# Causal attention cores: several heads' narrow score tiles in one bank, and value products in two visits a group

## The chip, the cores and the metric

The kernel runs on one core of a Trainium2 chip. Its time is the device time of one execution in microseconds; the profile is one execution taken by the hardware profiler. Of the core's engines, TensorE (PE) multiplies, VectorE (DVE), ScalarE (ACT) and GpSimd (POOL) do the element-wise work, and SyncE (SP) and ACT issue transfers. Matrix products land in eight banks of PSUM, each 512 fp32 columns wide. The engines run their own instruction streams in order and meet at semaphores.

## The reference

One decoder layer on x of 4 batches, 512 rows, 512 columns: causal self-attention (16 heads of 32), cross-attention to a context (32 heads of 16), then a second causal self-attention with rotary positions (16 heads of 32), then a gated mixture of experts. The change touches the cores of the two causal attentions:

```python
scores = jnp.einsum('bqhd,bkhd->bhqk', q, k)
scores = jnp.where(causal_mask[None, None], scores, NEG)
attn = jax.nn.softmax(scores, axis=-1)
out = jnp.einsum('bhqk,bkhd->bqhd', attn, v).reshape(b, s, HIDDEN)
return out @ w_out
```

## The kernel before

Phases follow one another: for each attention a projection phase and a core phase, then the experts. `core_phase` is built three times, as "first" and "rotary" (both causal) and as "cross". A causal core goes through 16 groups: four batches of four groups, a group being four heads of one batch. Each group has 16 steps; step i stands for key block m = i // 4 (128 keys) and head j = i % 4 of the group.

In each step PE first makes a tile of plain scores for a later group (`scores`, L1158), 26 steps ahead, into one of three banks (0, 1, 2). DVE takes that tile's row maxima with the mask added (`tile_max`, L1385), and only then is the bank free again: a tile of scores waits for the maximum of the tile three before it. When a group's 16 maxima are there, POOL splits them into two parts (`split_max`, L1584 and L1586), PE turns them at step 8 of the group before (`max_transpose`, L1172), ACT copies them out (L1311) and sends them with a transfer (`send_max`, L1093) into rows of the group's stack of queries. These rows subtract the maximum inside the product of the transposed scores, so step 0 of the group waits for the transfer.

Then the step makes its tile of transposed scores (`scoresT`, L1192): 128 keys by the queries from block m on, so 512, 384, 256 or 128 columns for m = 0, 1, 2, 3. A second product of 128 columns (L1195, the identity times a triangle of large negative numbers) adds the mask to the diagonal block. ACT takes the exponential out of the bank (L1339). These tiles share three banks (3, 4, 7) in turn with the turned maxima and with the output projection; `share_banks` replays the order and notes, for each use, the semaphore by which the bank's last user has left it.

The value products (`values`, L1233) take four heads side by side in four strips of 32 columns of the array, with fp32 operands; so do the products with a column of ones (L1201) that give the softmax's sums: one for query block 0 from the exponentials themselves (`sums_of_first`), one for blocks 1 to 3 (`sums`) from a total that POOL adds up (`add_keys`, L1566). I call a stretch in which PE leaves the wide products for such narrow strips a visit. A group's value products of blocks 0, 1, 2, 3 stand at its steps 9 and 13 and at steps 1 and 5 of the next group, the sums of block 0 behind the first of them and the other sums at step 4 of the next group: five visits. DVE turns the sums at step 5 (`flip_sums`, L1400), inverts them and turns them back at step 6 (L1407, L1410), and scales the values at step 7 (`scale`, L1420), between tile maxima. The next group's value product of block 0 waits for this scaling.

From its second batch on, a core also projects a finished batch in thirds of four products (`project`, L1250), in the second and third group of a batch: for tile m at steps 6, 7, 10 (m even) or 12, 14, 15 (m odd). I call these six groups of a core projecting groups and the other ten plain groups.

SP loads the stacks three groups ahead. A load waits until all transposed scores of the group that had the slot are done.

Of the kernel before, what the change touches and what calls it, by code (L numbers as in the profile page):

```python
# [24 lines left out]
P = 128  # L25
B, S, D = 4, 512, 512
# [888 lines left out]
def core_phase(nc, s, c, psum, a):  # L915
# [11 lines left out]
    with ctx:  # L927
# [56 lines left out]
        VALUES_LAG, SUMS_STEP = 7 if cross else 9, 4  # L984
# [18 lines left out]
        def values_behind(g, step):  # L1003

            n, beat = divmod(g * N16 + step - VALUES_LAG, HEADS_AT_ONCE)
            return divmod(n, TT) if beat == 0 and 0 <= n < GROUPS * TT else None
# [20 lines left out]
        def share_banks():  # L1027
# [14 lines left out]
            for g in range(GROUPS):  # L1042
                for step in range(N16):
                    n = g * N16 + step
                    whole(("score", n), "exp_done", n + 1)
# [12 lines left out]
        with nc.Fori(0, B // BODY) as loop:  # L1058
            rows = lambda m, bi: m[bass.ds((loop * BODY + bi) * S, S), :].rearrange("(t p) d -> p t d", p=P)
            with nc.Block() as block:  # L1060
# [86 lines left out]
                def _(pe):  # L1147
# [28 lines left out]
                    def scoresT(g, i):  # L1176

                        m, j = divmod(i, HEADS_AT_ONCE)
                        n, slot = g * N16 + i, g % STACK_SLOTS
                        at, r = j // HALVES, j % HALVES * HALF_ROWS  # L1180
                        bank, q0 = psum[bank_at["score", n]], start_k(m)
                        if i == 0:
# [95 lines left out]
                    for g in range(GROUPS):  # L1278
                        for step in range(N16):
# [6 lines left out]
                            if values_behind(g, step):  # L1286
                                g_v, m_v = values_behind(g, step)
                                values(g_v, m_v)
                                if causal and g_v == GROUPS - 1:
                                    sums_at_end(m_v)  # L1290
                                elif causal and m_v == 0:
                                    sums_of_first(g)
                            if causal and g and step == SUMS_STEP:
                                sums(g - 1)
                            if projected_at(g, step):
                                project(*projected_at(g, step))
                    for step in range(VALUES_LAG):
                        if values_behind(GROUPS, step):
                            g_v, m_v = values_behind(GROUPS, step)
# [6 lines left out]
                def _(act):  # L1306
# [18 lines left out]
                    for g in range(GROUPS):  # L1325
                        for step in range(N16):
                            n = g * N16 + step
                            q0 = start_k(step // HEADS_AT_ONCE)
                            act.wait_ge(s.scoresT_ready, n + 1)
# [1163 lines left out]
```

## Time and profile before

| what | us |
|---|---|
| median of 3 runs (lowest, highest) | 2136.97 (2126.91, 2140.46) |
| the profiled execution | 2134.5 |
| its span | 2132.7 |
| PE busy, share of the span | 1982.2, 93% |
| DVE busy | 1356.2, 64% |
| ACT busy | 1046.5, 49% |
| POOL busy | 706.1, 33% |

The two causal cores lie at about 176 to 432 us and 1184 to 1440 us. A matmul's busy time in the trace overlaps with its neighbours' (its end is modelled), so costs on PE are read from one start to the next. A row of the timeline may merge several records; x8 on a value product is four heads with two records each. A bracket such as [0.37 <-DVE ...] is time in which the engine sat idle before the row, and what ended it.

### The profile page before, as it was taken

The numbers are of one execution on the slowest core, as the hardware profiler recorded it, in microseconds if no ns is written. First come the engines' busy times: TensorE is split into PE (matmuls) and PEld (weight loads), VectorE is DVE, ScalarE is ACT, GpSimd is POOL, SyncE is SP. The second block draws the span as 40 slices with busy tenths as digits, with TensorE's granted clock in tenths as the row PEclk, the third lists the DMA queues.
The fourth block names the chain that finished last, engine by engine and source line by source line (L and its number), as shares of the span: only waits on it lengthen the run. The fifth ranks groups of instructions, "written<-read, shape, count | busy, mean of one in ns | idle before, by whom it ended". The sixth has DMA issues, their size and how long they took to land. (4 is left out here: it accounts for less than half of the span.)

```text
span 2132.7 us, 32709 instructions
## 1 busy us (share of the span) xinstructions
PE 1982.2 (93%) x10991; PEld 1385.6 (65%) x10991; DVE 1356.2 (64%) x2805; ACT 1046.5 (49%) x1890; POOL 706.1 (33%) x610
## 2 busy tenths in 40 slices
PE   7998999968789999998899899998999999999998
PEld 6875666656533334343777566666787888787876
DVE  6455666557689897976778566645331325577775
ACT  3424554445368676865443455534322221476775
POOL 0003655436512332323466465531000000143433
PEclk9998999989889999999999799998999999999999
DMA  5637676247665545443474867626120206434342
GB/s 202 223 141 183 149 170 153 91 163 268 233 180 119 141 113 140 119 104 95 188 242 181 203 153 164 149 81 245 45 99 1 79 25 254 171 67 76 64 77 37
DMA packets 151994, 297.75 MB, mean 140 GB/s; under 512 B 24722, under 2 KB 43284, under 8 KB 150740
## 3 DMA queue, kind: packets, MB, share of 16 engines
q1 hardware_dynamic: 114052, 242.29, 38.1%
q10 hardware_dynamic: 29040, 34.74, 6.0%
q0 software_dynamic: 8736, 18.62, 4.8%
q8 instruction: 89, 1.46, 0.3%
q14 instruction: 77, 0.63, 0.1%
HBM read 181.55 MB, written 102.50 MB: 133 GB/s over the span
## 5 line engine op out<-in xcount | busy, mean ns | idle before, releaser
L1339 ACT ACTIVATE cross_c_prob<-bank 128x512 f32<-128x512 f32 x512 | 271.1, 599 | 116.7 <-PE bank L1192 115.4
L1389 DVE TENSOR_REDUCE row_max<-bank 128x2 f32<-128x1024 f32 x248 | 290.6, 1211 | 27.6 <-PE bank L1158 26.6
L1859 PE MATMUL bank<-moe_hT,moe_w 128*128 128x512 f32 x1056 | 250.1, 393 | 7.7 <-DVE moe_w L2148 7.7
L1192 PE MATMUL bank<-stack 56*128 56x512 f32 (+4 forms) x768 | 232.9, 428 | 7.0 <-ACT cross_c_prob L1339 3.1
L1859 PEld LDWEIGHTS bank<-moe_hT,moe_w 128*128 128x128 f32 x1056 | 199.1, 189 | 50.1 <-issue 8.1
L1158 PE MATMUL bank<-stack 48*128 48x512 f32 (+4 forms) x720 | 190.7, 443 | 25.6 <-PEq L71 13.7
L1192 PEld LDWEIGHTS bank<-stack 56*128 56x128 f32 (+1 forms) x768 | 118.5, 193 | 136.4 <-ACT cross_c_prob L1339 69.6
L1339 ACT ACTIVATE first_c_prob<-bank 128x512 f32<-128x512 f32 (+3 forms) x256 | 106.1, 436 | 120.1 <-PE bank L1195 117.1
L1339 ACT ACTIVATE rotary_c_prob<-bank 128x512 f32<-128x512 f32 (+3 forms) x256 | 105.6, 436 | 117.8 <-PE bank L1195 115.2
L1385 DVE CUSTOM_DVE_ANT_0 first_c_masked<-bank,later 128x128 f32<-128x128 f32 (+3 forms) x240 | 108.8, 485 | 77.8 <-PE bank L1158 77.1
L1158 PEld LDWEIGHTS bank<-stack 48*128 48x128 f32 (+1 forms) x720 | 93.3, 196 | 98.4 <-DVE row_max L1389 45.1
L1385 DVE CUSTOM_DVE_ANT_0 rotary_c_masked<-bank,later 128x128 f32<-128x128 f32 (+3 forms) x240 | 108.5, 485 | 70.3 <-PE bank L1158 69.6
L2273 DVE TENSOR_TENSOR moe_prod<-moe_prod,bank 128x512 f32<-128x512 f32 x44 | 30.2, 687 | 179.2 <-PE bank L1859 179.2
L1233 PE MATMUL bank<-cross_c_prob,cross_c_v 128*32 128x512 f32 x1024 | 138.1, 612 | 0.6 <-DVE cross_c_flipped L1400 0.6
L1870 PE MATMUL bank<-moe_w,moe_inner 128*128 128x512 f32 x528 | 128.8, 393 | 0.0
L1797 POOL TENSOR_TENSOR moe_res<-moe_res,moe_x_tile 128x512 f32<-128x512 f32 x16 | 21.8, 1362 | 312.7 <-DMA moe_x_tile<-x 312.7
L1195 PE MATMUL bank<-earlier_r,ident_r 128*128 128x128 f32 x512 | 123.5, 242 | 0.0
L1817 POOL DMA_INDIRECT out_x<-moe_res,moe_token x39 | 61.8, 1585 | 173.1 <-ACT moe_res L2068 171.2
L1870 PEld LDWEIGHTS bank<-moe_w,moe_inner 128*128 128x128 f32 x528 | 98.7, 188 | 21.0
L2038 ACT ACTIVATE moe_prod<-bank 128x512 f32<-128x512 f32 x44 | 26.3, 598 | 172.6 <-PE bank L1859 172.6
L1969 PE MATMUL bank<-moe_down_w_e,moe_innerT 128*128 (+1 forms) x234 | 107.2, 593 | 1.5 <-issue 1.5
L1195 PEld LDWEIGHTS bank<-earlier_r,ident_r 128*128 128x128 f32 x512 | 101.6, 198 | 6.4
(402 smaller groups left out, 4482.6 us busy)
## 6 DMA issues: line engine op xcount, KB each, us to landing
qk_parts<-first_p_parts SPq DMA_DIRECT2D x32, 512.0 KB, 2.6
stack<-qk_parts SPq DMA_DIRECT2D x64, 256.0 KB, 6.4
qk_parts<-cross_p_parts SPq DMA_DIRECT2D x32, 512.0 KB, 2.6
stack<-qk_parts SPq DMA_DIRECT2D x256, 64.0 KB, 2.6
qk_parts<-rotary_p_parts SPq DMA_DIRECT2D x32, 512.0 KB, 2.7
moe_gate_up_e<-in_experts_gate_up SPq DMA_DIRECT2D x8, 1408.0 KB, 9.1
moe_raw<-in_shared_packed SPq DMA_DIRECT2D x11, 768.0 KB, 8.5
stack<-qk_parts SPq DMA_DIRECT2D x16, 512.0 KB, 5.3
```

What stands on the lines that cost most here:

```text
L1158: last = nc.tensor.matmul(bank[:, 0 : width_q(m)], q_stack[slot][r : r + PRODUCT_ROWS, at, m * P : (m + 1) * P], k_stack[slot][r : r + PRO ...
L1192: last = nc.tensor.matmul(bank[:, 0 : S - q0], k_stack[slot][r : r + ALL_ROWS, at, m * P : (m + 1) * P], q_stack[slot][r : r + ALL_ROWS, a ...
L1195: last = nc.tensor.matmul(bank[:, 0:P], c.ident_r[:], c.earlier_r[:], start=False, stop=True)
L1233: last = nc.tensor.matmul(psum[bank_o][32 * j : 32 * j + 32, q0:S], val, probability(g, m, j), start=m == 0, stop=m == TT - 1)
L1339: nc.scalar.activation(probability(g, step // HEADS_AT_ONCE, step % HEADS_AT_ONCE), psum[bank_at["score", n]][:, 0 : S - q0], ACT.Exp).the ...
L1385: nc.vector.tensor_tensor_reduce(out=masked[:, n % 2, 0 : width_q(m)], in0=bank[:, 0 : width_q(m)], in1=c.later[:, S - width_q(m) : S], sc ...
L1389: nc.vector.tensor_reduce(row_max[:, g % 2, m, j - 1 : j + 1], c.banks[:, first : first + WIDE, :], AX_X, ALU.max).then_inc(s.max_done, 1)
L1817: pool.indirect_dma_start(a.out, bass.IndirectOffsetOnAxis(ap=token[:, t : t + 1], axis=0), y[:, t % 2, :], None, bounds_check=B * S - 1, ...
L1859: last = nc.tensor.matmul(psum[bank][:], weights(pa, f, k), hT[p % 2][:, pb, k, :], start=m == 0, stop=m == len(steps) - 1)
L1870: last = nc.tensor.matmul(psum[SD[t]][:], inner[:, n % 2, pa, t * P : (t + 1) * P], w_d(pb, f), start=f == 0 and m == 0, stop=f == KF - 1 ...
L1969: last = nc.tensor.matmul(psum[6 + t % 2][:], innerT[0:kn, t % 2, n, :], rhs, start=n == 0, stop=n == len(FE_K) - 1)
L2273: nc.vector.tensor_tensor(prod[:], prod[:], psum[SU][:], ALU.mult).then_inc(s.s_inner, 1)
```

## The change

Tiles of transposed scores of key block 2 (256 columns) are made for two heads in one bank, those of block 3 (128 columns) for four heads in one bank. The bank gets one mask product for all its heads, of 256 or 512 columns (the triangle read again for each head), and one exponential of 512 columns. So steps 8, 10 and 12 lead, and steps 9, 11, 13, 14 and 15 make no transposed scores. The value products of blocks 0 and 1, with the sums of block 0, stand at step 13; those of blocks 2 and 3, with the other sums behind them, at step 4 of the next group. The cross-attention's order is as before.

```diff
+        PACKED = {2: 2, 3: 4} if causal else {}
+        heads_in = lambda step: PACKED.get(step // HEADS_AT_ONCE, 1)
+        leads = lambda step: step % heads_in(step) == 0
-        VALUES_LAG, SUMS_STEP = 7 if cross else 9, 4
+        VALUES_LAG = 7
+        VALUES_AT = {13: (0, (0, 1)), 4: (1, (2, 3))}
...
+            if causal:
+                back, tiles = VALUES_AT.get(step, (0, ()))
+                return [(g - back, m) for m in tiles if g >= back]
...
-                    whole(("score", n), "exp_done", n + 1)
+                    if leads(step):
+                        whole(("score", n), "exp_done", n + heads_in(step))
...
-                        last = nc.tensor.matmul(bank[:, 0 : S - q0], k_stack[slot][r : r + ALL_ROWS, at, m * P : (m + 1) * P],
-                                                q_stack[slot][r : r + ALL_ROWS, at, q0:S], start=True, stop=not causal)
+                        for h in range(heads):
+                            at, r = (j0 + h) // HALVES, (j0 + h) % HALVES * HALF_ROWS
+                            last = nc.tensor.matmul(tiles[:, h], k_stack[slot][r : r + ALL_ROWS, at, m * P : (m + 1) * P],
+                                                    q_stack[slot][r : r + ALL_ROWS, at, q0:S], start=h == 0, stop=not causal)
                         if causal:
-                            last = nc.tensor.matmul(bank[:, 0:P], c.ident_r[:], c.earlier_r[:], start=False, stop=True)
-                        last.then_inc(s.scoresT_ready, 1)
+                            last = nc.tensor.matmul(tiles[:, :, 0:P], c.ident_r[:], c.earlier_r[:].unsqueeze(1).to_broadcast([P, heads, P]), start=False, stop=True)
+                        last.then_inc(s.scoresT_ready, heads)
...
-                            if values_behind(g, step):
-                                g_v, m_v = values_behind(g, step)
+                            for g_v, m_v in values_behind(g, step):
                                 values(g_v, m_v)
                                 if causal and g_v == GROUPS - 1:
                                     sums_at_end(m_v)
-                                elif causal and m_v == 0:
-                                    sums_of_first(g)
-                            if causal and g and step == SUMS_STEP:
-                                sums(g - 1)
+                                elif causal and m_v == 1:
+                                    sums_of_first(g_v)
+                                elif causal and m_v == TT - 1:
+                                    sums(g_v)
...
+                            if causal and leads(step):
+                                nc.scalar.activation(prob_of[m][:, j : j + heads], psum[bank_at["score", n]][:, 0 : heads * (S - q0)].rearrange("p (h n) -> p h n", h=heads),
+                                                     ACT.Exp).then_inc(s.exp_done, heads)
```

PE before, from step 12's transposed scores to step 15 of a plain group (L1158 plain scores of the later group, L1192 transposed scores, L1195 mask, L1233 values of block 1):

```order
L1192 MATMUL bank<-first_q_stack,first_k_stack 128x128
L1195 MATMUL bank<-earlier_r,ident_r 128x128
L1158 MATMUL bank<-stack 128x256
L1192 MATMUL bank<-first_q_stack,first_k_stack 128x128
L1195 MATMUL bank<-earlier_r,ident_r 128x128
L1233 MATMUL bank<-first_c_prob,first_c_v 32x384 x4
L1158 MATMUL bank<-stack 128x384
L1192 MATMUL bank<-first_q_stack,first_k_stack 128x128
L1195 MATMUL bank<-earlier_r,ident_r 128x128
L1158 MATMUL bank<-stack 128x384
L1192 MATMUL bank<-first_q_stack,first_k_stack 128x128
L1195 MATMUL bank<-earlier_r,ident_r 128x128
```

PE with the change, from step 11 to step 0 of the next group (the same products are now L1166, L1204, L1207, L1245, and the sums L1213):

```order
L1166 MATMUL bank<-stack 128x256 x2
L1204 MATMUL bank<-first_q_stack,first_k_stack 128x128 x4
L1207 MATMUL bank<-earlier_r,ident_r 128x512
L1166 MATMUL bank<-stack 128x256
L1245 MATMUL bank<-first_c_prob,first_c_v 32x512 x4
L1245 MATMUL bank<-first_c_prob,first_c_v 32x384 x4
L1213 MATMUL bank<-first_c_prob,ones 32x128 x4
L1166 MATMUL bank<-stack 128x384 x3
```

The four masks of block 3 have become one, the four tiles stand together at step 12, and the values of block 0 have moved from step 9 to stand right ahead of those of block 1. Behind them three tiles of plain scores follow one another with nothing between.

PE before, steps 4 and 5 of a group (L1201 the sums, L1233 the values of block 3 of the group before; those of block 2 stood at step 1):

```order
L1158 MATMUL bank<-stack 128x512
L1192 MATMUL bank<-stack 128x384
L1195 MATMUL bank<-earlier_r,ident_r 128x128
L1201 MATMUL bank<-first_c_total,ones 32x384 x4
L1158 MATMUL bank<-stack 128x512
L1192 MATMUL bank<-stack 128x384
L1195 MATMUL bank<-earlier_r,ident_r 128x128
L1233 MATMUL bank<-first_c_prob,first_c_v 32x128 x4
```

PE with the change, steps 4 and 5:

```order
L1166 MATMUL bank<-stack 128x512
L1204 MATMUL bank<-first_q_stack,first_k_stack 128x384
L1207 MATMUL bank<-earlier_r,ident_r 128x128
L1245 MATMUL bank<-first_c_prob,first_c_v 32x256 x4
L1245 MATMUL bank<-first_c_prob,first_c_v 32x128 x4
L1213 MATMUL bank<-first_c_total,ones 32x384 x4
L1166 MATMUL bank<-stack 128x512
```

Three visits have become one at step 4: blocks 2 and 3 and the sums behind each other. The turn of the sums on DVE still follows at step 5, now behind the values of block 3 too.

## Rows read from the trace of the kernel before

**Rows 1.** the page, part 4: the chain of work that ended last, by engine.

```profile
PE 40%; DMA 1%; DVE 1%; issue 1%; POOL 1%; ACT 1%; SPq 0%; DVEq 0%; ACTq 0%; POOLq 0%
```

**Rows 2.** stretches from one turn of the maxima to the next: us, busy us of each engine.

```profile
core 0: us, PE busy (x) PEld busy (x) DVE busy (x) ACT busy (x) POOL busy (x), PEclk, DMA share, GB/s
354.51:367.17 12.66, 12.18 (x102) 8.22 (x101) 9.16 (x37) 7.40 (x19) 8.79 (x6) 1.00 0.96 213
367.17:381.45 14.28, 13.91 (x111) 9.72 (x110) 10.41 (x41) 7.75 (x19) 9.31 (x7) 1.00 0.40 90
381.45:399.04 17.59, 17.39 (x124) 12.45 (x124) 10.38 (x34) 7.84 (x18) 8.69 (x7) 1.00 0.46 148
```

**Rows 3.** PE in order of time, early plain group: start us, us, line, tiles, shape.

```profile
355.78 1.07 PE L1233 MATMUL bank<-first_c_prob,first_c_v 128*32 128x512 f32 x8 [0.37 <-DVE first_c_attn L1420]
356.63 0.43 PE L1201 MATMUL bank<-first_c_prob,ones 128*32 128x128 f32 x8
356.99 0.39 PE L1158 MATMUL bank<-stack 96*128 96x256 f32 x1
...
357.75 0.33 PE L1158 MATMUL bank<-stack 96*128 96x256 f32 x1
357.92 0.22 PE L1192 MATMUL bank<-first_q_stack,first_k_stack 104*128 104x128 f32 x1
357.98 0.28 PE L1195 MATMUL bank<-earlier_r,ident_r 128*128 128x128 f32 x1
358.09 0.33 PE L1158 MATMUL bank<-stack 96*128 96x256 f32 x1
...
358.33 0.27 PE L1195 MATMUL bank<-earlier_r,ident_r 128*128 128x128 f32 x1
358.53 0.85 PE L1233 MATMUL bank<-first_c_prob,first_c_v 128*32 128x384 f32 x8
359.31 0.45 PE L1158 MATMUL bank<-stack 96*128 96x384 f32 x1
359.59 0.23 PE L1192 MATMUL bank<-first_q_stack,first_k_stack 104*128 104x128 f32 x1
```

**Rows 4.** instruction groups by shape: weight loads of transposed scores; values of block 0.

```profile
L1192 PEld LDWEIGHTS bank<-stack 104*128 104x128 f32 x256 | 52.2, 204 | 5.5 <-DMA stack<-first_c_max_rows 2.0 <-DMA stack<-rotary_c_max_rows 1.4
...
L1233 PE MATMUL bank<-first_c_prob,first_c_v 128*32 128x512 f32 x128 | 18.8, 659 | 3.1 <-DVE first_c_attn L1420 2.6 <-ACT first_c_prob L1339 0.5
```

**Rows 5.** DVE in order of time, same group, from the turn of the sums.

```profile
352.34 0.72 DVE L1400 STREAM_TRANSPOSE first_c_flipped<-bank 128x512 f32<-128x512 f32 x1 [0.29 <-PE bank L1201]
...
353.60 0.29 DVE L1385 CUSTOM_DVE_ANT_0 first_c_masked<-bank,later 128x128 f32<-128x128 f32 x1
...
354.73 0.25 DVE L1385 CUSTOM_DVE_ANT_0 first_c_masked<-bank,later 128x128 f32<-128x128 f32 x1
...
354.94 0.69 DVE L1420 TENSOR_TENSOR first_c_attn<-bank,first_c_flipped 128x512 f32<-128x512 f32 x1
355.55 0.28 DVE L1385 CUSTOM_DVE_ANT_0 first_c_masked<-bank,later 128x128 f32<-128x128 f32 x1
...
357.42 0.42 DVE L1385 CUSTOM_DVE_ANT_0 first_c_masked<-bank,later 128x256 f32<-128x256 f32 x1 [1.37 <-PE bank L1158]
```

**Rows 6.** all engines in order of time: maxima split, then turned.

```profile
353.99 0.22 POOL L1586 TENSOR_TENSOR first_c_max_parts<-row_max,first_c_max_parts 128x16 fp32r<-128x16 f32 x1
...
354.51 0.60 PE L1172 MATMUL bank<-ident,first_c_max_parts 128*8 128x128 f32 x4
```

**Rows 7.** all engines in order of time: maxima sent, and who waited.

```profile
355.76 0.73 ACTq L1093 DMA_DIRECT2D stack<-first_c_max_rows  x1
...
360.67 0.19 PEld L1192 LDWEIGHTS bank<-stack 104*128 104x128 f32 x1 [0.37 <-DMA stack<-first_c_max_rows]
```

**Rows 8.** the same two operations one batch earlier.

```profile
292.31 0.71 ACTq L1093 DMA_DIRECT2D stack<-first_c_max_rows  x1
...
298.32 0.19 PEld L1192 LDWEIGHTS bank<-stack 104*128 104x128 f32 x1 [1.47 <-DMA stack<-first_c_max_rows]
```

More of the change, by code:

```diff
@@ L1003, in values_behind @@
         def values_behind(g, step):
+            if causal:
+                back, tiles = VALUES_AT.get(step, (0, ()))
+                return [(g - back, m) for m in tiles if g >= back]
             n, beat = divmod(g * N16 + step - VALUES_LAG, HEADS_AT_ONCE)
-            return divmod(n, TT) if beat == 0 and 0 <= n < GROUPS * TT else None
+            return [divmod(n, TT)] if beat == 0 and 0 <= n < GROUPS * TT else []
         def probability(g, m, j):
@@ L1176, in scoresT @@
                     def scoresT(g, i):
-                        m, j = divmod(i, HEADS_AT_ONCE)
-                        n, slot = g * N16 + i, g % STACK_SLOTS
-                        at, r = j // HALVES, j % HALVES * HALF_ROWS
+                        if not leads(i):
+                            return
+                        m, j0 = divmod(i, HEADS_AT_ONCE)
+                        n, slot, heads = g * N16 + i, g % STACK_SLOTS, heads_in(i)
                         bank, q0 = psum[bank_at["score", n]], start_k(m)
+                        tiles = bank[:, 0 : heads * (S - q0)].rearrange("p (h n) -> p h n", h=heads)
                         if i == 0:
@@ L1297, in _ @@
                     for step in range(VALUES_LAG):
-                        if values_behind(GROUPS, step):
-                            g_v, m_v = values_behind(GROUPS, step)
+                        for g_v, m_v in values_behind(GROUPS, step):
                             if causal:
@@ L1327, in _ @@
                             n = g * N16 + step
-                            q0 = start_k(step // HEADS_AT_ONCE)
-                            act.wait_ge(s.scoresT_ready, n + 1)
+                            m, j = divmod(step, HEADS_AT_ONCE)
+                            q0, heads = start_k(m), heads_in(step)
+                            if leads(step):
+                                act.wait_ge(s.scoresT_ready, n + heads)
                             if cross and n >= PROB_SLOTS:
@@ L1338, in _ @@
                                     act.wait_ge(s.sums_done, 2 * g - 1)
-                            nc.scalar.activation(probability(g, step // HEADS_AT_ONCE, step % HEADS_AT_ONCE), psum[bank_at["score", n]][:, 0 : S - q0],
-                                                 ACT.Exp).then_inc(s.exp_done, 1)
+                            if causal and leads(step):
+                                nc.scalar.activation(prob_of[m][:, j : j + heads], psum[bank_at["score", n]][:, 0 : heads * (S - q0)].rearrange("p (h n) -> p h n", h=heads),
+                                                     ACT.Exp).then_inc(s.exp_done, heads)
+                            if cross:
+                                nc.scalar.activation(probability(g, m, j), psum[bank_at["score", n]][:, 0:S], ACT.Exp).then_inc(s.exp_done, 1)
                             if step == MAX_STEP and g + 1 < GROUPS:
```

## The prediction

> **What bounds the kernel.** I read the chain of waits first: PE holds 40% of the span and no other engine or transfer over 1% (the rest is issue and small shares) [rows 1]. Next the stretches between two turns of the maxima in the first core's last batch: in a plain stretch of 12.66 us PE is busy 12.18, DVE 9.16; with output projection in it, 14.28 and 17.59 us, PE busy 13.91 and 17.39 [rows 2]. The reader is to see that PE sets the pace of a causal core, that DVE is at 72% of a plain stretch and at 59% of the longest, and that the clock is granted in full there. So time taken off PE counts, unless another engine is then late. Where that can be is read from the timelines of PE and DVE.
>
> **Mask products.** The kernel drops from 16 to 11 a group: four masks of 256-column tiles become two of 256 columns, four masks of 128-column tiles become one of 512. The columns streamed are the same, 16 x 128. So the gain is only what a narrow product costs beyond its columns. From mask to mask neighbours: plain scores of 256 columns, transposed scores of 128 and mask of 128 take 358.09 - 357.75 = 0.34 us for 512 columns [rows 3]; a value product of 512 columns in fp32 takes 0.85 us at four passes, so 512 columns are 0.21 us. That leaves 0.13 us for three products; weight loads with only 128 columns to hide behind show, one narrow product costing 0.11 us instead of 0.06. I price a mask at 0.11 us, 256 columns at 0.12 and 512 at 0.23. Then 8 x 0.11 - 2 x 0.12 - 0.23 = 0.41 us a group less. Bounds: 0 (only columns cost) and 0.55 (five products at 0.11). The four narrow score tiles in a row stay at 0.11 each, as now. I take 0.41, the price of the nearest rows.
>
> The Trainium skill, "TensorE: Matmul & The Clock Gate", section "Back-to-back issue gap", speaks against this term: its isolated gap is N/2.4 + 2.5 ns, by which eight masks of 128 columns and their three successors differ by some 12 ns a group. By that estimate the term would be 0; the 0.34 us of the row speaks against it.
>
> **Visits.** Five a group become two. Leaving one costs: values of 384 columns last 359.31 - 358.53 = 0.78 us to the next product, of which 0.64 is streaming (0.75 of 0.85), so 0.14; where sums follow values nothing is added (356.63 - 355.78 = 0.85). The 128-column sums show the same: 356.99 - 356.63 = 0.36, of which 0.21 is streaming. The first wide product after it is also late, 359.59 - 359.31 = 0.28 us for 384 columns against 0.22 that the 0.17 of 256 columns plus 0.05 would give. Entering costs 358.53 - 358.33 = 0.20 behind a mask worth 0.11 [rows 3]. Together 0.14 + 0.06 + 0.08 = 0.28 us a visit, 0.84 a group. Bounds 0.14 and 0.35 a visit.
>
> **The wait for the scaled values.** Values of block 0 waited 0.37 us for DVE's scaling [rows 3], 2.6 us in total in the first core [rows 4], which is seven times, so in plain groups. At step 13 the scaling is some 4 us old. This wait goes: 0.37 a plain group.
>
> **What comes late instead.** The visit at step 9 was also DVE's time to catch up. After the turn of the sums at 352.34 DVE works without a pause: maximum 0 at 353.60, maximum 1 at 354.73, the scaling at 354.94 to 355.55, then maxima 2 and 3 at 0.21 us each, done by 355.97; then it waits 1.37 us for PE, which is in the visit [rows 5]. With the change PE has no visit from step 5 to step 12. Each tile of scores waits for the maximum three before. The turn of the maxima cannot come earlier than the split of the last ones allows (POOL ends at 354.21, PE turned at 354.51 [rows 6]), so say 354.3. Then 0.36 for the turn and 0.11 for tile 3: tile 4 could start at 354.77, but maximum 1 is done at 354.94, and semaphore and weight load add some 0.15: 355.10, a wait of 0.33. Tile 4, two transposed tiles and a mask take 0.48: tile 5 at 355.58, maximum 2 is done at 355.76, so 355.91, 0.33 more. Tile 6 waits another 0.09. With 0.2 at the turn itself and 0.1 where tile 11 follows the three tiles in a row of steps 14, 15 and 0, that is 1.05 us in a plain group. Bounds: 0.4 (latency of a semaphore nothing) and 1.6 (every wait twice its latency). In projecting groups thirds of 0.9 us stand between these steps and cover them; I leave 0.1 us, for a bank that the projection holds.
>
> **The maxima's transfer.** It is issued 1.25 us behind the turn, 355.76 against 354.51, and in this group it released PE 4.9 us later, after a wait of 0.37 us [rows 6, 7]; in the batch before it took 6.0 us and PE waited 1.47 [rows 8]. In both causal cores weight loads of transposed scores waited 2.0 and 1.4 us on it [rows 4], so in most groups it had landed by the time PE came. PE came at 360.30 in rows 7 if it had not waited: 4.54 us behind the issue. With the change: 5.79 us from turn to step 0, less 0.37, 0.28 and 0.41, plus 0.75 of the new waits behind the turn: 5.48, or 4.23 behind the issue, 0.3 us less room. The groups that wait now lose 0.3 each, in all 2 us; the others nothing, or up to 0.3 if they land just in time. The stack loads that share the DMA engines can start earlier, since the last transposed scores now end at step 12, and so be out of the way earlier; I count nothing for that.
>
> The Trainium skill, "DMA: Bandwidth & Descriptors", section "Anatomy of one DMA", gives 2.0 us and bytes at 436 GB/s, an estimate of 2.2 us for these 64 KB; by it no group would wait. The 4.9 and 6.0 us of the trace disagree.
>
> **Other engines at no cost.** ACT's exponentials of block 2 and 3 become three of 512 columns instead of eight narrow ones; ACT is busy 7.40 of 12.66 us [rows 2] and loses work. The first exponential of block 2 is longer by 0.2 us ahead of the copy of the maxima, and ends before the turned maxima are there. The POOL totals end some 1 us before step 4's sums; the visit's values stand ahead of them. If that cover were gone, a late total would cost PE its lateness, once a group.
>
> **Sum.** Plain group: 0.41 + 0.84 + 0.37 - 1.05 = 0.57 us. Projecting group: 0.41 + 0.84 - 0.1 = 1.15. A core has ten and six: 5.7 + 6.9 = 12.6 us, two cores 25, less 2 for the transfer: 23 us. The profiled execution took 2134.5 us, so 2111.5; it lies 2.5 below the median of the three runs, inside their spread. I forecast **2111 us**, 1.2% less. About 1% (21 us, so 2116) is what a measurement of this kernel can tell from no change.
>
> **Rivals.**
> - Full gain: the waits on maxima do not come, because DVE's order leaves PE just behind it. For: DVE has 28% to spare on average. Against: the pauseless stretch of rows 5. Gain 2 x (10 x 1.62 + 6 x 1.25) - 2 = 45 us: 2089. Chance 0.12.
> - DVE eats the plain groups: waits of 1.6 us leave nothing of 1.62 there, and only projecting groups gain, 2 x 6.9 = 14 us, less the 2: 2122. For: three banks only, and each late release also uncovers a weight load. Chance 0.18.
> - The merged masks do nothing, as the columns are the same. Then 32 x 0.41 = 13 us less gain: 2124. For: equal columns, and a triangle read four times with a stride of zero, which no row shows. Against: the 0.34 us. Chance 0.14.
> - Slower: the maxima's transfer becomes the bound. Its place is step 0, and from 4.23 us behind the issue on each us is PE's. If the earlier stack loads now fall on it in every plain group and it takes the 6.0 us of rows 8, 20 groups wait 1.8 us, 36 us against the 25 gained: 2146. Turning point: 5.5 us. At 7 us it would be 20 x 2.8 - 25 = 31 slower, 2166. Against: only three or so groups a core wait now, and loads start earlier. Chance 0.08.
> - Forecast: 0.48.
>
> **Chances and range.** Faster by over 1% (below 2116): 0.41 of the forecast, the full gain 0.12, 0.03 of the masks' case: 0.56. Slower by over 1%: 0.04. The rest, 0.40, is within. The range runs from near the full gain to short of the slower case, 2092 to 2131: it leaves out most of the slower case, part of the full gain, and the worst of DVE's bound.
>
> **What would show it.** In the profile after: 352 mask products, their mean below 0.3 us; two runs of L1245 a group, the second with sums at its end; no wait of PE on the scaled values; waits of L1166's weight loads on row maxima longer in total than before, at steps 8 to 12 of plain groups; plain stretches near 12.0 us and stretches with projection 1 to 1.4 us shorter. I would be wrong if PE's idle time at step 0 grows by a us, or if plain stretches stay at 12.6.

## The result, and the profile after

| | median of the runs, us | lowest, highest |
|---|---|---|
| before | 2138.72 (4 runs) | 2126.91, 2142.66 |
| the change | 2106.87 (4 runs) | 2101.05, 2111.76 |

The ratio is 0.9859, 95% interval 0.9812 to 0.9906: 30 us faster by the ratio. The same kernel was measured once more, with six runs, beside three of the experiments.

> The change itself once more, on the same chip as the three runs beside it. Ratio to before 0.983 to 0.989. If the length of its waits for the maxima's transfer is a matter of one execution, the records show another sum than the 10 us of the first profile.

It took 2109.24 us, ratio 0.9882 (0.9857 to 0.9907). Its record shows 6.2 us of PE waiting for the maxima's transfer in the causal cores, where the first one shows 10.2 (below): the sum of these waits differs by 4 us between two executions of one kernel, so a single record of another kernel says little by it. The profiled execution that is shown in the following is the slowest of the first four, 2111.76 us with a span of 2110.0.

The page's line of the engines (busy us, share, instructions), and of its part 4 the chain of work that ended last:

```profile
PE 1963.1 (93%) x10831; PEld 1381.2 (65%) x10831; DVE 1353.1 (64%) x2805; ACT 1022.5 (48%) x1730; POOL 706.1 (33%) x610
PE 40%; DMA 2%; issue 1%; DVE 1%; POOL 1%; ACT 1%; SPq 0%; DVEq 0%; ACTq 0%; POOLq 0%
```

PE is busy 19.1 us less than before (1982.2, with 160 products more), and the span is 22.7 us shorter. It still holds 40% of the chain, and DMA has 2% where it had 1 [rows 1].

Stretches from one turn of the maxima to the next, in the first core, in a view restricted to PE: the stretch, its length, PE's busy us (and instructions), granted clock, DMA engines' share, GB/s. First the kernel before, in stretches without a wait for the maxima's transfer: a plain one, the one into the first projecting group, and the two projecting ones.

```profile
230.57:242.87 12.30, 11.93 (x102) 1.00 0.86 194
242.87:256.97 14.10, 13.73 (x110) 1.00 0.87 204
320.44:338.37 17.93, 17.73 (x127) 1.00 0.49 117
338.37:354.51 16.14, 15.94 (x118) 1.00 0.53 134
```

The same four kinds with the change, and behind them the plain stretch that ends a batch, at 347.52 us:

```profile
233.18:244.91 11.73, 11.53 (x98) 1.00 0.75 171
244.91:258.32 13.41, 13.21 (x105) 1.00 0.89 193
316.16:332.68 16.52, 16.45 (x121) 1.00 0.49 121
332.68:347.52 14.84, 14.77 (x113) 1.00 0.56 146
347.52:362.18 14.66, 13.19 (x98) 0.88 1.08 219
```

The first four are 12.30, 14.10, 17.93 and 16.14 us before and 11.73, 13.41, 16.52 and 14.84 after: 0.57, 0.69, 1.41 and 1.30 less, 3.97 in a batch of four groups. The fifth is 14.66 long, its clock is granted at 0.88, and it was 12.66 before [rows 2]: two us worse. Each of the four kinds gets shorter where there is no wait for the transfer; some of the stretches that have one get longer.

PE in that last plain group, from the turn of the maxima to the next group's first transposed scores (x2 and x4 are tiles that the view has merged):

```profile
347.52 0.60 PE L1180 MATMUL bank<-ident,first_c_max_parts 128*8 128x128 f32 x4
347.88 0.77 PE L1166 MATMUL bank<-stack 96*128 96x128 f32 x2
348.49 0.40 PE L1204 MATMUL bank<-first_q_stack,first_k_stack 104*128 104x256 f32 x2
348.72 0.28 PE L1207 MATMUL bank<-earlier_r,ident_r 128*128 128x256 f32 x1
349.10 0.59 PE L1166 MATMUL bank<-stack 96*128 96x256 f32 x2
349.54 0.56 PE L1204 MATMUL bank<-first_q_stack,first_k_stack 104*128 104x128 f32 x4
349.93 0.45 PE L1207 MATMUL bank<-earlier_r,ident_r 128*128 128x512 f32 x1
350.21 0.28 PE L1166 MATMUL bank<-stack 96*128 96x256 f32 x1
350.42 1.71 PE L1245 MATMUL bank<-first_c_prob,first_c_v 128*32 128x512 f32 x16
351.95 0.40 PE L1213 MATMUL bank<-first_c_prob,ones 128*32 128x128 f32 x8
352.28 0.79 PE L1166 MATMUL bank<-stack 96*128 96x384 f32 x3
354.37 0.50 PE L1204 MATMUL bank<-stack 104*128 104x512 f32 x1 [1.30 <-DMA stack<-first_c_max_rows]
```

DVE at the same time: maximum 1, the scaling, maximum 2:

```profile
347.94 0.25 DVE L1400 CUSTOM_DVE_ANT_0 first_c_masked<-bank,later 128x128 f32<-128x128 f32 x1
...
348.15 0.69 DVE L1435 TENSOR_TENSOR first_c_attn<-bank,first_c_flipped 128x512 f32<-128x512 f32 x1
348.76 0.28 DVE L1400 CUSTOM_DVE_ANT_0 first_c_masked<-bank,later 128x128 f32<-128x128 f32 x1
...
348.96 0.08 DVE L1400 DVE_READ_ACCUMULATOR2_ANT row_max<- 128x1 f32 x1
```

The merged row at 347.88 holds tiles 3 and 4 of plain scores, and the next row begins at 348.49: 0.61 us for two narrow tiles priced at 0.11 each. Tile 4 waited for maximum 1, done when the scaling starts at 348.15. Tile 5 follows the mask of 348.72 and was due 0.12 later, at 348.84; it stands at 349.10, behind maximum 2, whose last row starts at 348.96. Tiles 5 and 6 then take 0.44 to the next row instead of 0.24, as tile 6 waits for maximum 3. These are the three waits of the forecast's list: 0.39, 0.26 and 0.20 us by the distances of starts, against 0.33, 0.33 and 0.09. At 352.28 three tiles of 384 columns run on, and PE then stands idle 1.30 us for the transfer.

The groups by shape (count | busy us, mean ns | idle us ahead): the value products of block 0, which waited for DVE 2.6 us [rows 4] and do so no more, and the masks:

```profile
L1245 PE MATMUL bank<-first_c_prob,first_c_v 128*32 128x512 f32 x128 | 17.9, 633 | 0.1
...
L1207 PE MATMUL bank<-earlier_r,ident_r 128*128 128x128 f32 x256 | 60.3, 235 | 0.0
L1207 PE MATMUL bank<-earlier_r,ident_r 128*128 128x256 f32 x64 | 18.8, 294 | 0.0
L1207 PE MATMUL bank<-earlier_r,ident_r 128*128 128x512 f32 x32 | 14.9, 465 | 0.0
```

The masks are 352, with a mean of (60.3 + 18.8 + 14.9) / 352 = 0.27 us, where 512 had one of 0.24. PE's waits for the maxima's transfer over the whole execution: us in total, times, longest.

```profile
PE bank L1204 <- DMA stack<-first_c_max_rows: 5.5, 3, 3.2
PE bank L1204 <- DMA stack<-rotary_c_max_rows: 4.7, 3, 1.9
PE bank L1204 <- DMA stack<-cross_c_max_rows: 1.3, 3, 0.8
```

That is 10.2 us in six waits of the causal cores; before, the same two lines had 1.2 and 0.6 us, in one wait each. Four of the six stand at the ends of the second and third batch of each core (0.96, 1.30, 1.88 and 1.37 us, 5.5 together). The other two, 3.20 and 1.47 us, stand at the second group of each core, where there was none before. The longer one:

```profile
195.47 0.65 PE L1204 MATMUL bank<-stack 104*128 104x512 f32 x1 [3.20 <-DMA stack<-first_c_max_rows]
```

The stretch of turns around it takes 18.52 us where it took 13.40, which is the largest single loss in this record; in the second record of the change it takes 14.40, without such a wait.

### The profile page after: what moved, and what is told of

Read it like the earlier page. It is cut to its first block and busy times, and to the rows that moved or that the text cites. A ratio compares the mean times of both kernels' runs of the same rounds, so it can differ in the third digit from the quotient of the medians.

```text
span 2110.0 us, 32325 instructions
## 1 busy us (share of the span) xinstructions
PE 1963.1 (93%) x10831; PEld 1381.2 (65%) x10831; DVE 1353.1 (64%) x2805; ACT 1022.5 (48%) x1730; POOL 706.1 (33%) x610
## 5 line engine op out<-in xcount | busy, mean ns | idle before, releaser
L1204 PE MATMUL bank<-stack 56*128 56x512 f32 (+4 forms) x768 | 224.0, 433 | 15.0 <-DMA stack<-first_c_max_rows 5.5
L1166 PE MATMUL bank<-stack 48*128 48x512 f32 (+4 forms) x720 | 184.7, 442 | 26.9 <-PEq L71 13.5
L1204 PEld LDWEIGHTS bank<-stack 56*128 56x128 f32 (+1 forms) x768 | 114.3, 195 | 143.7 <-ACT cross_c_prob L1355 69.1
L1352 ACT ACTIVATE rotary_c_prob<-bank 128x512 f32<-128x512 f32 (+1 forms) x176 | 94.1, 559 | 122.4 <-PE bank L1207 122.1
L1352 ACT ACTIVATE first_c_prob<-bank 128x512 f32<-128x512 f32 (+1 forms) x176 | 94.0, 558 | 120.9 <-PE bank L1207 118.2
L1166 PEld LDWEIGHTS bank<-stack 48*128 48x128 f32 (+1 forms) x720 | 92.7, 197 | 90.9 <-DVE row_max L1404 46.1
L1245 PE MATMUL bank<-cross_c_prob,cross_c_v 128*32 128x512 f32 x1024 | 137.2, 608 | 0.6 <-DVE cross_c_flipped L1415 0.6
L1207 PE MATMUL bank<-earlier_r,ident_r 128*128 128x128 f32 (+2 forms) x352 | 94.0, 267 | 0.0
L2328 DVE SCALAR_TENSOR_TENSOR moe_chunks<-moe_gate_up_e,moe_w_ln,moe_chunks 128x704 fp32r<-128x704 f32 x78 | 74.0, 951 | 27.0 <-ACT moe_chunks L2098 26.7
```

Source lines behind the costliest of these rows:

```text
L1166: last = nc.tensor.matmul(bank[:, 0 : width_q(m)], q_stack[slot][r : r + PRODUCT_ROWS, at, m * P : (m + 1) * P], k_stack[slot][r : r + PRO ...
L1204: last = nc.tensor.matmul(tiles[:, h], k_stack[slot][r : r + ALL_ROWS, at, m * P : (m + 1) * P], q_stack[slot][r : r + ALL_ROWS, at, q0:S] ...
L1207: last = nc.tensor.matmul(tiles[:, :, 0:P], c.ident_r[:], c.earlier_r[:].unsqueeze(1).to_broadcast([P, heads, P]), start=False, stop=True)
L1245: last = nc.tensor.matmul(psum[bank_o][32 * j : 32 * j + 32, q0:S], val, probability(g, m, j), start=m == 0, stop=m == TT - 1)
L1352: nc.scalar.activation(prob_of[m][:, j : j + heads], psum[bank_at["score", n]][:, 0 : heads * (S - q0)].rearrange("p (h n) -> p h n", h=he ...
```

## Experiments

Ratios are to the kernel before, with 95% intervals. The stretches named are those of the four kinds above, in that order, without a wait for the transfer.

**Only the packing.**

```diff
-        VALUES_LAG = 7
-        VALUES_AT = {13: (0, (0, 1)), 4: (1, (2, 3))}
+        VALUES_LAG, SUMS_STEP = 7 if cross else 9, 4
...
-            if causal:
-                back, tiles = VALUES_AT.get(step, (0, ()))
-                return [(g - back, m) for m in tiles if g >= back]
```

> Shared banks, merged masks and exponentials as in the change, but the value products and sums at their old steps (five visits a group). If a narrow mask product costs more than its columns, as the forecast priced it (0.41 us a group), this is 13 us faster than before, 2125 against 2138, ratio 0.994, and PE's waits on row maxima stay near those of before, since the visit at step 9 still covers DVE. If only columns cost, it is within 3 us of before, ratio 0.999 to 1.001.

Measured: 2114.78 us, 0.992 (0.9888 to 0.9951), 17 us faster; weight loads of plain scores waited 51.3 us on row maxima, near the 47.8 of before. A plain and a projecting stretch of it, and its value products of block 0:

```profile
230.81:243.11 12.30, 11.77 (x98) 1.00 0.77 176
316.62:333.63 17.01, 17.01 (x121) 1.00 0.52 127
```

```profile
L1242 PE MATMUL bank<-first_c_prob,first_c_v 128*32 128x512 f32 x128 | 17.9, 631 | 5.0 <-DVE first_c_attn L1432 4.5 <-ACT first_c_prob L1349 0.5
```

A plain stretch gains nothing: PE arrives at step 9 earlier, and the wait for the scaled values grows from 2.6 to 4.5 us. The gain is in the projecting stretches, 17.93 to 17.01. PE's waits there for the copies of finished output tiles, 1.4 us a core in six waits before, are gone from its list, 0.23 us a projecting group. By that the 0.21 us which merged masks save in a plain group (the run with one mask product a head, below) go into the wait for the scaled values, which grew by 1.9 us over the ten plain groups of a core.

**Only the two visits.**

```diff
-        PACKED = {2: 2, 3: 4} if causal else {}
+        PACKED = {}
```

> Two visits a group as in the change, but every head's transposed tile in its own bank with its own mask and exponential. If the forecast's price of a visit (0.28 us) and of the waits that take their place holds, this is 12 to 18 us faster than before, ratio 0.992 to 0.994. If the visits' gain is wholly eaten by waits on row maxima and on the maxima's transfer, it is within 4 us of before.

Measured: 2123.4 us, 0.9958 (0.9938 to 0.9978), 9 us faster (5 to 13 by the interval): less than the 12 to 18 expected and more than the rival's 4, with an interval that only touches the first and just misses the second. Its plain and projecting stretches:

```profile
228.47:240.55 12.08, 11.79 (x101) 1.00 0.88 197
317.21:334.61 17.40, 17.18 (x126) 1.00 0.51 121
```

Plain 12.08, projecting 17.40. The four kinds together: packing alone gives 1.93 us a batch, visits alone 1.49 (12.08, 13.63, 17.40 and 15.87), both together 3.97. In a plain stretch neither does much alone, 0 and 0.22, and both give 0.57: each alone leaves PE at a wait that both together don't have. With the packing alone it is the scaled values. With the visits alone PE's list has 4.0 us in 15 waits for row maxima of the causal cores, which neither before nor the change has, and still the 2.8 us for copies of output tiles. That these waits are the whole of the difference was read from the lists and not tested.

**One mask product a head.**

```diff
-                            last = nc.tensor.matmul(tiles[:, :, 0:P], c.ident_r[:], c.earlier_r[:].unsqueeze(1).to_broadcast([P, heads, P]), start=False, stop=True)
+                            for h in range(heads):
+                                last = nc.tensor.matmul(tiles[:, h, 0:P], c.ident_r[:], c.earlier_r[:], start=False, stop=h == heads - 1)
```

> The change with shared banks and merged exponentials, but the mask product made for each head by itself (128 columns each, 16 a group instead of 11). If the narrow products' overhead is what the packing brings on PE, this loses 13 us against the change: 2120, ratio to before 0.992. If the columns alone cost, or if what packing brings is fewer waits on banks and on ACT, it stays at 2107, ratio 0.986.

Measured: 2115.8 us, 0.9907 (0.9878 to 0.9936). Stretches 11.94, 13.67, 16.87 and 15.21: 0.21, 0.26, 0.35 and 0.37 longer than the change's, 0.30 on average. So five mask products cost 0.30 us at equal columns, 0.06 each, and 0.07 each in the projecting stretches, where PE is hardly interrupted. By the stretches that is some 9 us in 32 groups, where 13 were expected. The time agrees, 9 us over the first median of the change and 7 over the second, but the intervals overlap; the stretches decide.

**One more visit.**

```diff
-        VALUES_AT = {13: (0, (0, 1)), 4: (1, (2, 3))}
+        VALUES_AT = {13: (0, (0,)), 14: (0, (1,)), 4: (1, (2, 3))}
```

> The change with the value products of block 1 (and the sums behind them) one step later than those of block 0, so that one tile of plain scores stands between: three visits a group instead of two, everything else as it was. By the forecast's price a stretch without a transfer wait gets 0.28 us longer, 9 us in all: ratio to before 0.991. If only the drain of 0.14 us counts, because the product behind a visit is late for its weights anyway, it is 0.14 a stretch, 4 us, 0.989.

Measured (four runs): 2110.23 us, 0.9891 (0.9844 to 0.9939), too near to the change for the time to tell. The stretches tell: 16.82 and 15.14 in projecting groups, 0.30 more each; 11.82 and 13.52 in the others, 0.10 more each. The additional visit costs 0.30 us in the projecting stretches and 0.1 in the others. That it costs less there because the next tiles wait for maxima anyway is an explanation and not shown.

**Small stack loads.**

```diff
         n = next(sent)
+        if t.causal and g >= STACK_SLOTS:
+            last, src = first + 1, src[0:1]
```

> The change, with each load of a causal stack from the fifth group on shrunk to its first row (the later groups so compute on the first groups' stacks; the output is not the reference's). If the maxima's transfer is late because the stack loads share the DMA engines with it, PE's waits on it (10 us in the two cores' records) vanish, with the slow clock behind them: 8 to 14 us faster than the change, ratio to before 0.980 or so. If the transfer's own latency is the bound, the waits stay and the time is that of the change, 0.986.

Measured: 2099.75 us, 0.9844 (0.9813 to 0.9875), 7 us less than the change's first median and 3 by the ratios, 9 and 8 against the second, with the intervals overlapping. That is the lower end of the expected 8 to 14 us or short of it, and its interval leaves out the 0.980. The waits did vanish: in its record PE waits for no transfer of the causal cores, neither at the ends of batches nor at their start, and the plain stretch that ends a batch has the length of any other:

```profile
343.26:354.96 11.70, 11.52 (x97) 1.00 0.29 77
```

11.70 instead of 14.66 us, and the DMA engines' share at 0.29 instead of 1.08. The transfer's own latency leaves PE no wait; with the full loads beside it there is one.

**The scaling three steps later.**

```diff
-        FLIP_STEP, NORM_STEP, BACK_STEP = (4, 6, 8) if cross else (5, 6, 7)
+        FLIP_STEP, NORM_STEP, BACK_STEP = (4, 6, 8) if cross else (5, 6, 10)
```

> The change with DVE's scaling of the values at step 10 instead of 7, so that maxima 2 and 3 of a group no longer stand behind it. If PE's waits for those maxima are what the change gave back in plain groups (0.46 us at tiles 5 and 6), a plain stretch without a transfer wait goes from 11.7 to 11.3 us and 20 groups give 6 to 9 us, unless PE then stands at the maxima's transfer: ratio to before 0.982. If those waits are hidden by something else, no change against the run beside it.

Measured: 2111.35 us, 0.9888 (0.9861 to 0.9916), the same as the change beside it (0.9882). Its plain stretches without and with a wait for the transfer:

```profile
231.25:242.59 11.34, 11.24 (x98) 1.00 0.77 163
346.02:362.08 16.06, 14.19 (x98) 0.79 1.07 209
```

The waits for maxima 2 and 3 are gone where they were expected (11.34 against 11.73), and the end of a batch takes it back: 16.06 against 14.66, at a granted clock of 0.79, with waits for the transfer of 9.1 us in the causal cores. The stretches gain as expected. The expected 0.982 lies outside the interval; the record shows the gain going into the transfer.

**Earlier turn of the maxima.**

```diff
-        MAX_STEP = 9 if cross else 8
+        MAX_STEP = 9 if cross else 6
...
-out=x1, lead=10, **layer)
+out=x1, lead=12, **layer)
```

> The change with the plain scores two steps further ahead (28 instead of 26) and the turn of the maxima at step 6 instead of 8, so that their transfer is issued some 0.9 us of PE work earlier. If the room between the transfer's issue and step 0 is short by what the records show (10 us of waits, and the slow clock behind the longest), the waits drop to a third and this is 6 to 10 us faster than the change: ratio 0.981. If the transfer is late for a reason that moves with it, or if PE now waits for the split of the maxima instead, nothing or a loss of a few us.

Measured: 2102.61 us, 0.9862 (0.9839 to 0.9885); waits for the transfer 5.2 us instead of the 6.2 of the change beside it, which is no drop to a third and within what two executions differ by. It is 7 us below the change beside it only by medians, and the two intervals overlap. PE's waits for POOL's split, one in each core, grew from 4.7 us to 6.7, as the rival said.

**Both.** 

> Scaling at step 10 and the earlier turn together. If both theories hold and the two do not share one wait, their gains add: 12 to 18 us faster than the change, ratio 0.978. If the earlier turn alone mattered, as the run with it alone.

Measured: 2102.46 us, 0.9858 (0.9834 to 0.9882). The gains do not add: its waits for the transfer are 8.2 us, more than the 6.2 of the change beside it, and those for POOL's split 6.1. That PE with its shorter stretches comes to the transfer earlier is the likely reason; the expected 0.978 is outside the interval.

**Stores behind the loads.** Where the change's waits at the ends of batches come from is in SP's own rows. SPq is SP's queue; L1119 is the store of a projected tile, L213 a stack's loads (five a stack; the first of one stack is shown and the first of the next), ACTq's L1101 the maxima's transfer; the last row is the weight load of PE that it released:

```profile
335.94 6.58 SPq L1119 DMA_DIRECT2D x<-first_c_out_t  x2
342.56 0.59 SPq L213 DMA_DIRECT2D first_q_stack<-qk_parts  x1
...
348.87 0.73 ACTq L1101 DMA_DIRECT2D stack<-first_c_max_rows  x1
...
350.41 0.59 SPq L213 DMA_DIRECT2D first_q_stack<-qk_parts  x1
...
354.37 0.19 PEld L1204 LDWEIGHTS bank<-stack 104*128 104x128 f32 x1 [1.61 <-DMA stack<-first_c_max_rows]
```

The same time by stretches of PE, columns as above:

```profile
340.00:343.00 3.00, 3.00 (x17) 1.00 0.00 0
346.00:355.00 9.00, 7.53 (x60) 1.00 1.09 240
357.00:359.00 2.00, 2.00 (x20) 0.50 1.06 208
```

SP's row of two stores lasts from 335.94 to 342.52: the second one waits for a tile whose last third is projected at step 15 of the batch's third group, and the next stack's loads are issued behind it, at 342.56. From 340 to 343 the DMA engines move no byte. From 346 to 355 they are full (share 1.09), with the loads of the stack after it issued 7.9 us later, at 350.41. The maxima's transfer, issued at 348.87 between the two, releases PE 5.5 us later. Behind the wait PE gets half its clock for 357 to 359, the level of 1.2 GHz.

Before, the loads of the same two stacks were issued so:

```profile
349.30 0.59 SPq L213 DMA_DIRECT2D first_q_stack<-qk_parts  x1
...
360.36 0.59 SPq L213 DMA_DIRECT2D first_q_stack<-qk_parts  x1
```

The first came 5.2 us ahead of the turn at 354.51, with the change 5.0: behind the store it gains nothing from slots that are free at step 12. The second came 4.6 us behind the transfer's issue, and with the change comes 1.5 behind it. The transfer itself hardly changed: at the four batch ends of the two cores it released PE 4.9 to 6.0 us behind its issue before, 5.4 on average, and 5.2 to 6.1 with the change, 5.6 on average. What shrank is PE's way: the weight load of step 0 would have come 4.54 us behind the issue before, and comes 3.89 behind it with the change, at each of the four places.

```diff
                             next_stack(sp, g + 3)
+                        if causal and g > G and OUT_AT[3][-1][0] >= (g - 1) % G >= OUT_AT[1][-1][0]:
+                            store(sp, ((g - 1) // G - 1) * TT + [m for m in range(TT) if OUT_AT[m][-1][0] == (g - 1) % G][-1])
...
-                        for m in early:
+                        for m in early[:-1] if causal else early:
```

> The change with SP's second store of each projecting group (which waits for the output of step 10 or 15) put behind the next stack's loads instead of ahead of them. In the change's record SP waits in that store from 336 to 342.5 us, no byte moves from 340 to 343, and then two stacks' loads fall on the maxima's transfer. If that is what makes the transfer late at the end of a batch, the stretches of 14.7 us there go to 12 to 13, four or so in the two cores: 5 to 9 us faster than the change, ratio 0.983. If the loads merely take their 1.5 MB a group wherever they start, nothing.

Measured: 2094.55 us, 0.9831 (0.9797 to 0.9864), the ratio that was expected: 12 and 15 us below the change's two medians, 6 and 11 by the ratios, with intervals that overlap. SP's and ACT's rows at the same place:

```profile
328.90 0.59 SPq L213 DMA_DIRECT2D first_q_stack<-qk_parts  x1
...
334.75 0.34 SPq L1119 DMA_DIRECT2D x<-first_c_out_t  x1
...
341.45 0.73 ACTq L1101 DMA_DIRECT2D stack<-first_c_max_rows  x1
...
342.98 0.59 SPq L213 DMA_DIRECT2D first_q_stack<-qk_parts  x1
```

A stack's loads now start 11.2 us ahead of the turn of the maxima (328.90 against 340.10; 5.0 in the change), ahead of the store of 334.75, and 14.1 us before those of the next stack. At the issue of the maxima's transfer, 341.45, the DMA engines have little else to do (share 0.07 from 341.4 to 343.0, where it is over 1 at this place in the change), and the stretch at the end of the batch is an ordinary one, 11.76 us instead of 14.66:

```profile
340.10:351.86 11.76, 11.57 (x98) 1.00 0.76 174
```

The other three batch ends are the same, 11.75 to 11.77 us, where the change has 12.75 to 16.58 in its first record and 12.87 to 14.45 in its second. PE waits at none of them. The move doesn't touch the wait at the second group of a core; in this record it is 1.7 us in the second core and nothing in the first.

**All three.** 

> Scaling at step 10, plain scores two further ahead with the turn at step 6, and the stores behind the loads. If the transfer is the bound once PE has been relieved, this adds the gains the two former runs could not show: ratio 0.979 to 0.982, 2090 to 2095. If the loads' bytes are the bound in any order, it stays at 2102, ratio 0.986.

Measured: 2089.76 us, 0.9803 (0.9768 to 0.9837): 42 us under the kernel before by the ratio, as expected. Its ratio is below both intervals of the change (0.9812, 0.9857 at their lower ends), though its own interval still overlaps the first a little. This is the fastest by its median of the versions that compute everything; the run with the stores alone is within its interval. A projecting and a plain stretch:

```profile
321.35:337.50 16.15, 16.15 (x121) 1.00 0.69 167
337.50:348.54 11.04, 11.04 (x97) 1.00 0.69 149
```

Only the plain one can be held against those above: with the turn at step 6 a stretch holds other thirds of the projection.

**Both moves with small loads.** 

> Scaling at step 10 and the earlier turn, with the causal stack loads from the fifth group on shrunk to their first row (the output is not the reference's). If the loads are the only thing that stands against those two moves, PE never waits for the transfer and the plain stretches are all 11.0 to 11.3 us: ratio 0.975 to 0.979, 8 us or more below the run with both moves. If PE is then held by something else, it is no better than the change with small loads, 0.984.

Measured: 2091.55 us, 0.981 (0.9777 to 0.9843), short of the 0.979, and 11 us below the run with both moves, as expected. Its plain stretches are 11.03 us as expected, but it has no more to gain in the steady part than the kernel with all three; one wait of 4.6 us for POOL's split in each core's first groups is what it still has.

## Why the prediction was right

The forecast was 2111 us and 1.2% less; measured were 2107 and 1.4%. Its range held the time. The terms for PE's own work are borne out in kind, but the nearness of the sum is partly luck: more was gained in the projecting groups than forecast and more lost at the transfer.

- **Mask products**, 0.41 us a group: measured 0.30 (0.21 in plain, up to 0.37 in projecting ones). Right that columns are not all; but the merged mask of block 3 takes 0.28 us to the next start (349.93 to 350.21) where I had 0.23, half of what is missing. The rival by which merged masks do nothing is refuted. The Trainium skill's isolated gap ("TensorE: Matmul & The Clock Gate", section "Back-to-back issue gap") makes this term an estimate of next to nothing; the trace does not agree, with its 0.30. The same section says that the isolated gap counts too little for narrow products in a stream, and gives 81 ns at 128 columns and 131 ns at 512 there, which the forecast left out. By these, with 256 columns between the two, the term is an estimate of 0.26 to 0.36 us. The 0.30 agrees with that difference, though not with the two figures: the rows have 0.11 us [rows 3] and 0.28.
- **Visits**, 0.28 us each: an additional one costs 0.30. The trace agrees with the term's unit. Three fewer did not give 0.84 everywhere: from packing alone to the full change a projecting stretch gains 0.49 and 0.30 us, where the forecast's terms give 0.74. What stands in the rest was not found.
- **The wait for the scaled values**, 0.37: gone. That packing alone makes it longer was not foreseen.
- **The waits on maxima**, 1.05: at tiles 4, 5 and 6 the changed kernel shows them in the places given, 0.85 us for the three where I had 0.75, and putting the scaling later took 0.39 back in a plain stretch. Wrong was one sign named for it: weight loads' waits on row maxima would grow in total, I said. In the causal cores they fell, from 21.2 + 13.3 + 13.3 = 47.8 us to 11.5 + 8.2 + 7.1 = 26.8. Where a wait ends is the better sign than a sum.
- **A term that was missing**: with eleven tiles of scores a group in place of sixteen, PE hardly waits for a copy of a projected tile to free a bank: 2.8 us in both cores before, 0.4 now. Packing alone gives a projecting stretch 0.92 and 1.00 us, of which masks are 0.35 and 0.37 and the bank's waits 0.23; 0.34 and 0.40 are left unexplained. The projecting stretches so gained 1.41 and 1.30 where I had 1.15, the stretch between the two kinds 0.69. A batch came to 3.97 us against 3.44 of the forecast (plain 0.57, as forecast to the hundredth, which is partly luck, as its terms were each off).
- **The transfer**, 2 us: this term of the sum was mis-sized. PE waited 10.2 us for it in the profiled execution, against 1.8 before, and 6.2 in the one profiled later. Three things were off. PE's way to step 0 lost 0.65 us at the ends of batches (4.54 to 3.89) where I had 0.3. I counted nothing for stack loads that start earlier, in the belief that they are out of the way sooner. At the end of a batch the first set can't be earlier, as it stands behind a store. At the second group of a core the next stack's loads now start 1.6 us behind the transfer's issue (189.60 against 188.00, and 1182.91 against 1181.33) where they started over 5 behind it, and there the waits of 3.20 and 1.47 us are new. With those loads made small they are gone, but no run moved these loads alone, and the second record has only the one of 1.8 us. And the slower clock behind a wait was not in the term. The rival "slower" named the place and this mechanism rightly; the release came 5.2 to 6.1 us behind the issue at the ends of batches, around its turning point, but in most groups PE doesn't wait. The forecast's estimate of 2.2 us rests on a fit that the Trainium skill ("DMA: Bandwidth & Descriptors", section "Anatomy of one DMA") gives for transfers issued by GpSimd. These are issued by ACT.

How the stretches add up: a batch with projection gained 3.97 us and the first batch, which has none, four times 0.57. That is 14.2 us a core and 28.4 in two, where the forecast had 25. In the profiled executions the causal phases, from the end of their projection to their last product, are 264.6 and 260.4 us before, 254.0 and 254.4 after, 16.6 together. Of the 12 us between, 8.4 are the waits for the transfer (10.2 less 1.8). The rest fits the lower clock behind these waits: the stretch of 14.66 us is 2.93 over a plain one, with 1.30 of waiting in it, and a granted clock of 0.88 in 14.66 us is 1.76 us of full clock lost, about the 1.63 that remain. That last step is worked out and not measured. In the second record of the change the two phases are 250.1 and 251.0 us, 24 less than before: 4 of the 7.5 us between the two records of the change are the waits. The two spans of the first comparison differ by 22.7 us, so 6 came from phases that the change doesn't touch; how much of the 30 us of the medians is of that kind is open.

## What to carry to other kernels

Price a removed switch of the array's shape or a narrow product by start-to-start distances, then ask which wait stood behind it: here each half of the change alone left PE at waits that the two together don't have. When the bounding engine gets faster, look next at the queue that starts the transfers: a store that waits for a late result, ahead of loads whose slot has been free for 6 us, cost 1 to 5 us at each batch end here. Loads that can start earlier need not be out of the way sooner: ask what they now fall on. And a gain on one engine that a transfer takes back shows in the stretches without that transfer, before it shows in the time.

## What the runs showed of the hardware

- Idle time of PE was followed by a slow clock: behind the 1.30 us wait for the transfer the granted clock was 0.88 over the stretch, and 0.79 in the run with the later scaling, behind 1.79 us. Behind the 3.20 us wait it was 0.50 from 196 to 202 us. The stretches shown that have no such wait had 1.00.
- The 64 KB transfer of the maxima released PE 5.5 us behind its issue with the DMA engines' share at 1.09, and left no wait in the stretch with the share at 0.29, nor in one at 0.76 where the share was 0.07 at its issue.
- A mask of 512 columns, whose moving operand is read again for each head (a stride of zero), takes 0.28 us to the next start in the rows of PE above (349.93 to 350.21), where the forecast had 0.23. Whether the stride or the strided output makes the 0.05 was not tried.
